# Attention on one core: both score pairs ahead of the value group in the step behind a turn

## The chip, the cores and the metric

The kernel runs on one core of a Trainium2 chip. The metric is the device time of one execution in microseconds (us), the median over several runs. Engines are named as in the profile: PE is TensorE (PEld its weight loads), ACT ScalarE, DVE VectorE, POOL GpSimd, SP SyncE.

## The reference, cut to what matters

The program is a chain of four residual layers on a stream of 4096 tokens of width 256 (two batches of 2048): a linear attention, a mixture of eight experts with two per token, a softmax attention and a second mixture of experts. The change touches only the softmax attention, the third layer:

```python
q = proj_h(v @ Wq.T)            # 16 heads of 16, first component sqrt(1 + |rest|^2)
k = proj_h(v @ Wk.T)
vv = (v @ Wv.T) as heads
sc = (-q0 k0 + q[1:] . k[1:]) / dh ** 0.5
at = softmax(sc, axis=-1)       # over 2048 keys, not causal
out = at @ vv
```

## The kernel before, in words

The function `attention` works on 16 head pairs (two heads of one batch; `NPAIR`, eight pairs for each batch), one after the other. A pair has 32 steps (`ST`): 16 key tiles of 128 keys for the first half of the queries, then the same 16 for the second half. What a step does is called by its place in the loop of L1774:

- `scores(p, step, 0)` and `scores(p, step, 1)` (L1701): two score pairs. Each is two matmuls, one per head on its own half of the rows, 128 keys by 512 queries, into one unit of `psS`, two banks of PSUM. ACT turns each unit into its exponentials (L1800), 128 x 1024 at a time, so 64 in a head pair. In this text exp 20.1 is the one of the second score pair of step 20, and the same for the others.
- `weigh(p, step - 2)` (L1711): the value group, four matmuls side by side in columns of 32 (eight records in the trace), that multiply the exponentials of two steps ago with the values and add them up in `psO`. `pexp` has six buffers, so an exp also waits for the value group that reads the exps of three steps back.
- `means(q, n)` (L1727): one product for the next head pair's shift (an upper estimate of the scores' maximum), which DVE reduces (L1816). It is not there in the last steps of the fifteenth pair and in the sixteenth, since no pair follows.

`psS` has three units (`RING`), given out in turn by the list that `uses` writes (L1577). Three times in a head pair the list puts something else between the scores: behind step 3 the transposed output of the pair before (`turn_out`, L1757; not in the first pair), behind step 19 that of the first half of this pair (`turn_out`), and behind step 28 the transposed shift of the next pair (`turn_shift`, L1750; not in the last pair). These are the turns. `unit_free` (L1691) makes each use wait for the end of what had the same unit three places earlier in the list. For a score pair in a step without a turn that is the score pair three before. In the step behind a turn, the first score pair waits for the first exp of the step before, and the second score pair for the second exp of the step before. `OUT` is (19, 3) and `TURN` 28.

TensorE carries out its instructions in the order of the code, each behind its own wait.

Of the kernel before, what the change touches and what calls it, by code (L numbers as in the profile page):

```python
# [1512 lines left out]
def attention(nc, k):  # L1513
# [18 lines left out]
    TURN = ST - 4  # L1532
    OUT = (KT16 + 3, 3)
# [7 lines left out]
    with Stage(nc, "at") as s:  # L1541
# [53 lines left out]
        def shift_place(p):  # L1595

            bank = psS[:, unit["shift", p, 0], :] if p else psM[:, :]
            return bank.bitcast(F16)[0:ST, 0:P]

        def early(at):  # L1600

            return psS[:, at % RING, :].rearrange("p (h c) -> p h c", h=2)

        def keys(stack, p):
            return stack[:, p % HPAIR, p // HPAIR * TS:(p // HPAIR + 1) * TS]
# [4 lines left out]
        def mean_at(p, step):  # L1610
            return p + 1 + (step + AHEAD) // ST, (step + AHEAD) % ST

        with nc.Block() as block:

            @block.gpsimd
            def _(pool):
                def take_v(p):
                    pool.tensor_copy(vst[:, p % 2, :, :, 0:D],  # L1618
                                     batch(p)[:, :, p % HPAIR * 2 * D:(p % HPAIR + 1) * 2 * D].rearrange("p t (h d) -> p h t d", h=2)
                                     ).then_inc(v_ready, 1)  # L1620

                pool.memset(vst[:, :, :, :, :], 0.0).then_inc(start, 1)
                pool.wait_ge(start, 1)
                pool.memset(vst[:, :, :, :, D:D + 1], 1.0).then_inc(start, 1)
                pool.wait_ge(start, 2)
                def high(c):
                    pool.wait_ge(raw_in[c % SR], (c // SR + 1) * 16)
                    if c >= SR:

                        pool.wait_ge(w_out[c % SR], c // SR * 16)  # L1630
                    pool.tensor_scalar(part(c, 0), raw(c), scale(c), 1.0, ALU.mult, ALU.mult).then_inc(w_high, 1)  # L1631

                take_v(0)
                take_v(1)
                for p in range(2, NPAIR + 1):
                    if p < NPAIR:

                        pool.wait_ge(weighed, 6 + (p - 1) * ST * 2)
                        take_v(p)
                    if p > HPAIR:  # L1640
                        for c in range((p - 1 - HPAIR) * NSP, (p - HPAIR) * NSP):
                            high(c)
# [46 lines left out]
            @block.tensor  # L1689
            def _(pe):  # L1690
                def unit_free(use):  # L1691

                    v = place[use]
                    if v >= RING:
                        kind, p, n = order[v - RING]
                        if kind == "score":
                            pe.wait_ge(raised, p * ST * 2 + n + 1)
                        else:
                            pe.wait_ge(x_free, x_use[kind, p, n] + 1)

                def scores(p, step, n):  # L1701
                    kt, c = step % KT16, step // KT16 * 2 + n
                    use = "score", p, step * 2 + n
                    unit_free(use)
                    for hh in range(2):
                        r = slice(hh * HR, (hh + 1) * HR)
                        mm = pe.matmul(psS[:, unit[use], hh * BANK:(hh + 1) * BANK], keys(k.KT, p)[r, kt * P:(kt + 1) * P],  # L1707
                                       keys(k.QT, p)[r, c * BANK:(c + 1) * BANK], start=True, stop=True)
                    mm.then_inc(scored, 1)

                def weigh(p, step):  # L1711
                    kt, y = step % KT16, step // KT16

                    pe.wait_ge(raised, (p * ST + step) * 2 + 2)
                    if kt == 0:
                        if 2 * p + y:

                            pe.wait_ge(o_out, 2 * p + y)
                        pe.wait_ge(v_ready, p + 1)
                    for g in range(4):  # L1720
                        n, hh = g // 2, g % 2
                        mm = pe.matmul(psO[g * VW:(g + 1) * VW, :], vst[:, p % 2, hh, kt, :],  # L1722
                                       pexp[:, (p * ST + step) % 3 * 2 + n, hh * BANK:(hh + 1) * BANK],
                                       start=(kt == 0), stop=(kt == KT16 - 1))
                    mm.then_inc(weighed, 2)

                def means(p, n):  # L1727
                    if n == 0:
                        pe.wait_ge(k_ready, 4 * (p + 1))
                    if p * ST + n:  # L1730

                        pe.wait_ge(reduced, p * ST + n)
                    hh, t = n % 2, n // 2
                    r = slice(hh * HR, (hh + 1) * HR)
                    pe.matmul(psM[:, :], keys(k.QT, p)[r, t * P:(t + 1) * P], ksumT[r, p % 2, :],  # L1735
                              start=True, stop=True).then_inc(maxed, 1)

                def first_means(p, t):
                    at = p * KT16 + t
                    if t == 0:  # L1740
                        pe.wait_ge(k_ready, 4 * (p + 1))
                    if at >= 3:

                        pe.wait_ge(reduced, 2 * (at - 3) + 2)
                    for hh in range(2):
                        r = slice(hh * HR, (hh + 1) * HR)
                        pe.matmul(early(at)[:, hh, :], keys(k.QT, p)[r, t * P:(t + 1) * P], ksumT[r, p % 2, :],
                                  start=True, stop=True).then_inc(maxed, 1)

                def turn_shift(p):  # L1750
                    pe.wait_ge(shifted, p + 1)
                    if p:
                        unit_free(("shift", p, 0))
                    pe.transpose(shift_place(p), shift[:, :, :].rearrange("p h t -> p (h t)"),
                                 k.identh[:, :]).then_inc(x_turned, 1)

                def turn_out(p, y):  # L1757
                    pe.wait_ge(o_out, 2 * p + y + 1)
                    unit_free(("out", p, y))
                    for c in range(4):  # L1760
                        mm = pe.transpose(psS[:, unit["out", p, y], c * P:(c + 1) * P], oT[:, y, c * P:(c + 1) * P], k.ident[:, :])
                    mm.then_inc(x_turned, 1)

                pe.wait_ge(start, 2)
                for t in range(KT16):
                    first_means(0, t)
                turn_shift(0)
                for t in range(AHEAD // 2):
                    first_means(1, t)

                pe.wait_ge(reduced, ST + AHEAD)
                for p in range(NPAIR):
                    pe.wait_ge(shift_in, 32 * (p + 1))
                    for step in range(ST):  # L1774
                        scores(p, step, 0)
                        if step >= 2:
                            weigh(p, step - 2)
                        elif p:
                            weigh(p - 1, ST - 2 + step)
                        scores(p, step, 1)  # L1780
                        q, n = mean_at(p, step)
                        if q < NPAIR:
                            means(q, n)
                        if step == OUT[1] and p:
                            turn_out(p - 1, 1)
                        if step == OUT[0]:
                            turn_out(p, 0)
                        if step == TURN and p + 1 < NPAIR:
                            turn_shift(p + 1)
                weigh(NPAIR - 1, ST - 2)  # L1790
                weigh(NPAIR - 1, ST - 1)
                turn_out(NPAIR - 1, 1)
# [590 lines left out]
```

## Time and profile before

| | us |
|---|---|
| median of 3 runs | 2340.03 (2338.78 to 2341.39) |
| the profiled execution, its own time | 2340.75 |
| its span | 2339.0 |
| PE busy | 2034.9 (87%) |
| ACT busy | 1513.5 (65%) |
| DVE busy | 1365.6 (58%) |
| exponentials of the attention, L1800, 1024 of them | 942.7 |

The span is what the profile covers; the execution's own time is 1.75 us longer. Times in the rows below are counted from the start of the span. In a row of the timeline several instructions of one kind that follow each other without a gap are merged: the first number is the start of the first, the second the time up to the end of the last, and the count stands behind the x.

### The profile page before, as it was taken

To read this page: it belongs to the slowest core of one execution; us is meant where nothing else is said; L and a number is where in the kernel's file an instruction comes from. 1 tells how busy PE (TensorE), PEld (TensorE's weight loads), DVE (VectorE), ACT (ScalarE), POOL (GpSimd) and SP (SyncE) were. 2 spreads that over 40 slices of the span, in tenths; PEclk is the share of its full clock that TensorE was granted. 3 is DMA by queue.
4 is the path that set the end of the run, shared out by engine and by line. 5 is a ranking of instruction groups with operands and counts; after the bars stand their busy time and mean duration, and the time that the engine had idled before them with its cause. 6 is when DMAs were issued, how large, how long until landed. Compare 5 with 4: busy or idle time off the path is not lost. (4 is left out here: it accounts for less than half of the span.)

```text
span 2339.0 us, 43032 instructions
## 1 busy us (share of the span) xinstructions
PE 2034.9 (87%) x13329; PEld 970.5 (41%) x13330; DVE 1365.6 (58%) x3004; ACT 1513.5 (65%) x2495; POOL 463.8 (20%) x395
## 2 busy tenths in 40 slices
PE   5997799960996999999999999999863699999994
PEld 3786555540662222222222222222252467667663
DVE  5567544438787444444445555554147787777773
ACT  2215333324674999999999999999963344444442
POOL 0030277752000000000000000000000143344341
PEclk9998899985997999999999999999986799999997
DMA  5006377763100000000002222222174477767774
GB/s 200 1 1 225 82 154 152 151 149 154 43 29 1 1 2 1 1 2 1 1 19 73 73 73 73 73 73 73 55 243 148 173 178 174 173 174 174 172 173 129
DMA packets 157317, 225.11 MB, mean 96 GB/s; under 512 B 14080, under 2 KB 130992, under 8 KB 157184
## 3 DMA queue, kind: packets, MB, share of 16 engines
q1 hardware_dynamic: 129376, 184.04, 25.3%
q0 software_dynamic: 27264, 37.24, 9.4%
q10 hardware_dynamic: 544, 2.10, 0.3%
q8 instruction: 78, 1.28, 0.2%
q14 instruction: 55, 0.45, 0.1%
HBM read 157.63 MB, written 65.57 MB: 95 GB/s over the span
## 5 line engine op out<-in xcount | busy, mean ns | idle before, releaser
L1800 ACT ACTIVATE at_pexp<-at_psS 128x1024 f32<-128x1024 f32 x1024 | 942.7, 1163 | 30.7 <-PE at_psS L1707 30.7
L1816 DVE TENSOR_REDUCE at_mx<-at_psM 128x1 f32<-128x512 f32 x474 | 327.3, 691 | 413.8 <-PE at_psM L1735 410.2
L1722 PE MATMUL at_psO<-at_pexp,at_vst 128*32 128x512 f32 x4096 | 546.0, 605 | 3.5 <-ACT at_pexp L1800 0.8
L1707 PE MATMUL at_psS<-l1c_QT,l1c_KT 64*128 64x512 f16 x2048 | 412.7, 385 | 16.2 <-ACT at_pexp L1800 9.8
L1707 PEld LDWEIGHTS at_psS<-l1c_QT,l1c_KT 64*128 64x128 f16 x2048 | 105.4, 93 | 536.5 <-ACT at_pexp L1800 498.6
L2149 PE MATMUL ex_psH<-wide_wgu,ex_xT 128*128 x1278 | 259.9, 357 | 0.6 <-issue 0.6
L986 POOL DMA_INDIRECT sums<-ex_y,top_dst x107 | 170.0, 1589 | 280.1 <-ACT ex_y L2205 226.6
L2220 DVE SCALAR_TENSOR_TENSOR ex_bias<-ex_psH,top_w_scale,ex_bias 128x456 f32<-128x456 f32 x213 | 147.4, 692 | 76.6 <-PE ex_psH L2149 60.3
L2193 ACT ACTIVATE ex_sg<-ex_bias 128x228 f32<-128x228 f32 x213 | 83.7, 393 | 152.3 <-DVE ex_bias L2220 152.3
L972 POOL DMA_INDIRECT ex_xg<-normed,top_tok x142 | 140.1, 987 | 197.6 <-POOLq L81 148.7
L1735 PE MATMUL at_psM<-at_ksumT,l1c_QT 64*128 64x512 bf16 x474 | 178.8, 377 | 0.0
L2149 PEld LDWEIGHTS ex_psH<-wide_wgu,ex_xT 128*128 128x128 f16 x1278 | 124.5, 97 | 112.2 <-issue 4.0
L1722 PEld LDWEIGHTS at_psO<-at_pexp,at_vst 128*32 128x32 f32 x4096 | 81.7, 108 | 186.9 <-issue 120.4
L2172 PE MATMUL ex_psY<-wide_w2h,ex_hT 114*128 x1278 | 151.3, 273 | 1.1 <-DVE ex_y L2247 0.7
L1058 PE MATMUL ex_psH<-l_w,ex_xT 128*128 x284 | 142.7, 626 | 0.0
L1618 POOL COPY at_vst<-wide_x 128x512 f32<-128x512 f32 x16 | 9.7, 610 | 656.4 <-PE at_psO L1722 656.4
L2172 PEld LDWEIGHTS ex_psY<-wide_w2h,ex_hT 114*128 114x128 f16 x1278 | 124.4, 98 | 15.8 <-issue 1.6
L1126 DVE TENSOR_SCALAR ex_y<-ex_psY,top_wgt 128x256 f32<-128x256 f32 x71 | 34.3, 483 | 134.6 <-PE ex_psY L1075 124.5
L1095 ACT ACTIVATE ex_hT<-ex_psG 128x256 f32<-128x256 f32 x71 | 27.2, 383 | 123.0 <-PE ex_psG L1067 123.0
L2205 ACT ACTIVATE ex_y<-ex_y,top_wgt 128x256 f32<-128x256 f32 x71 | 36.1, 508 | 93.7 <-DVE ex_y L2247 93.7
L2231 DVE TENSOR_TENSOR ex_h<-ex_bias,ex_sg 128x228 f32<-128x228 f32 x213 | 82.8, 389 | 11.2 <-ACT ex_sg L2193 11.2
L1631 POOL TENSOR_SCALAR l1c_KT<-l1c_KT,top_w_scale 128x684 f16<-128x684 f32 (+1 forms) x48 | 40.9, 858 | 227.8 <-DMA l1c_KT<-in_L_ffn_W 215.0
(359 smaller groups left out, 2735.8 us busy)
## 6 DMA issues: line engine op xcount, KB each, us to landing
ex_bias<-in_L_ffn_bg SPq DMA_DIRECT2D x71, 342.0 KB, 4.7
ex_bias<-in_L_ffn_b SPq DMA_DIRECT2D x71, 342.0 KB, 5.5
ex_piece<-in_L_ffn_W SPq DMA_DIRECT2D x48, 228.0 KB, 2.7
l1c_KT<-in_L_ffn_W SPq DMA_DIRECT2D x32, 342.0 KB, 3.4
halves<-l1c_KT SPq DMA_DIRECT2D x32, 342.0 KB, 3.2
wide_wgu<-halves SPq DMA_DIRECT2D x8, 1368.0 KB
ex_b<-in_L_ffn_b SPq DMA_DIRECT2D x71, 128.0 KB
normed<-rt_area SPq DMA_DIRECT2D x16, 512.0 KB, 2.6
```

What stands on the lines that cost most here:

```text
L972: pool.indirect_dma_start(xg[:, g, :], None, k.xn_d, bass.IndirectOffsetOnAxis(k.tok[:, t:t + 1].bitcast(U32), 0)).then_inc(got[g], 16)
L986: pool.indirect_dma_start(sums[t % len(sums)], where, y[:, j, :], None, compute_op=ALU.add).then_inc(put[j], 16)
L1058: mm = pe.matmul(psH[:, j, :], xT[:, j, kk, :], k.w13[:, ds(eh, 1), kk, :].rearrange("p a c -> p (a c)"), start=(kk == 0), stop=(kk == KC ...
L1707: mm = pe.matmul(psS[:, unit[use], hh * BANK:(hh + 1) * BANK], keys(k.KT, p)[r, kt * P:(kt + 1) * P], keys(k.QT, p)[r, c * BANK:(c + 1) * ...
L1722: mm = pe.matmul(psO[g * VW:(g + 1) * VW, :], vst[:, p % 2, hh, kt, :], pexp[:, (p * ST + step) % 3 * 2 + n, hh * BANK:(hh + 1) * BANK], s ...
L1735: pe.matmul(psM[:, :], keys(k.QT, p)[r, t * P:(t + 1) * P], ksumT[r, p % 2, :], start=True, stop=True).then_inc(maxed, 1)
L1800: act.activation(pexp[:, u % 6, :], psS[:, unit["score", u // (ST * 2), u % (ST * 2)], :], ACT.Exp, scale=D ** -0.5 / (QS * QS)).then_inc( ...
L1816: dve.tensor_reduce(mx[:, n:n + 1], psM[:, :], AX.X, ALU.max).then_inc(reduced, 1)
L2149: mm = pe.matmul(psH[:, n, 0:G2].rearrange("p (n c) -> p n c", n=2), xT[:, j, x, kk, :], k.wgu[:, ds(e, 1), kk, :, w, n * HW:(n + 1) * HW] ...
L2172: mm = pe.matmul(psY[:, 0:C], hT[:, j, x, g, :], k.w2h[:, ds(e, 1), w, g, :].rearrange("p a c -> p (a c)"), start=(at == 0), stop=(at == l ...
L2193: act.activation(sg[:, n, :], bias[:, st.slot(1, BR), n, 0, :], ACT.Silu).then_inc(gated, 1)
L2220: dve.scalar_tensor_tensor(hb, psH[:, n, 0:G2].rearrange("p (n c) -> p n c", n=2), k.w_scale[:, 1:2], hb, ALU.mult, ALU.add).then_inc(adde ...
```

## The change

In the step behind a turn (`turned`: step 20, step 29, and from the second pair on step 4), the second score pair is issued right behind the first, ahead of the value group. In all other steps the order is as before. Step 29 of the last pair is also reordered, though no turn stands ahead of it: 47 steps in all. Nothing is added or taken away, and the list of units is the same.

```diff
                 for p in range(NPAIR):
                     pe.wait_ge(shift_in, 32 * (p + 1))
                     for step in range(ST):
+                        turned = step - 1 in (OUT[0], TURN) or (step - 1 == OUT[1] and p)
+
                         scores(p, step, 0)
+                        if turned:
+                            scores(p, step, 1)
                         if step >= 2:
                             weigh(p, step - 2)
                         elif p:
                             weigh(p - 1, ST - 2 + step)
-                        scores(p, step, 1)
+                        if not turned:
+                            scores(p, step, 1)
                         q, n = mean_at(p, step)
                         if q < NPAIR:
                             means(q, n)
```

PE in the step behind a turn of the output (here step 20 of the first pair); `at_psS<-l1c_QT,l1c_KT` are scores, `at_psO` the value group, `at_psM` the means product:

```order
 L1735 MATMUL at_psM<-at_ksumT,l1c_QT 128x512
 L1761 MATMUL at_psS<-top_ident,at_oT 128x128 x4
-L1707 MATMUL at_psS<-l1c_QT,l1c_KT 128x512 x2
-L1722 MATMUL at_psO<-at_pexp,at_vst 32x512 x4
-L1707 MATMUL at_psS<-l1c_QT,l1c_KT 128x512 x2
+L1707 MATMUL at_psS<-l1c_QT,l1c_KT 128x512 x4
+L1722 MATMUL at_psO<-at_pexp,at_vst 32x512 x4
 L1735 MATMUL at_psM<-at_ksumT,l1c_QT 128x512
 L1707 MATMUL at_psS<-l1c_QT,l1c_KT 128x512 x2
```

The four score matmuls of the step now stand together, and the value group comes between them and the means product.

PE in the step behind the turn of the shift (step 29 of the first pair):

```order
 L1735 MATMUL at_psM<-at_ksumT,l1c_QT 128x512
 L1754 MATMUL at_psS<-top_identh,at_shift 32x128
-L1707 MATMUL at_psS<-l1c_QT,l1c_KT 128x512 x2
-L1722 MATMUL at_psO<-at_pexp,at_vst 32x512 x4
-L1707 MATMUL at_psS<-l1c_QT,l1c_KT 128x512 x2
+L1707 MATMUL at_psS<-l1c_QT,l1c_KT 128x512 x4
+L1722 MATMUL at_psO<-at_pexp,at_vst 32x512 x4
 L1735 MATMUL at_psM<-at_ksumT,l1c_QT 128x512
 L1707 MATMUL at_psS<-l1c_QT,l1c_KT 128x512 x2
```

The same move behind the one transposition of the shift.

## Rows read from the trace of the kernel before

**Rows 1.** The page, costliest groups: busy, mean ns of one | idle before, releaser.

```profile
L1800 ACT ACTIVATE at_pexp<-at_psS 128x1024 f32<-128x1024 f32 x1024 | 942.7, 1163 | 30.7 <-PE at_psS L1707 30.7
L1816 DVE TENSOR_REDUCE at_mx<-at_psM 128x1 f32<-128x512 f32 x474 | 327.3, 691 | 413.8 <-PE at_psM L1735 410.2
```

**Rows 2.** Timeline of ACT, exp 4.1 of the third pair to 4.0 of the fourth.

```profile
872.12 58.92 ACT L1800 ACTIVATE at_pexp<-at_psS 128x1024 f32<-128x1024 f32 x64 [0.17 <-PE at_psS L1707]
```

**Rows 3.** Timeline of ACT, eighth pair, exp 4.1 alone and exps 4.1 to 19.1.

```profile
1167.58 1.02 ACT L1800 ACTIVATE at_pexp<-at_psS 128x1024 f32<-128x1024 f32 x1 [0.17 <-PE at_psS L1707]
...
1167.58 28.52 ACT L1800 ACTIVATE at_pexp<-at_psS 128x1024 f32<-128x1024 f32 x31 [0.17 <-PE at_psS L1707]
```

**Rows 4.** Timeline of PE, eighth pair, from the turn behind step 19 to step 21.

```profile
1194.41 0.63 PE L1761 MATMUL at_psS<-top_ident,at_oT 128*128 128x128 f32 x4
1195.24 0.39 PE L1707 MATMUL at_psS<-l1c_QT,l1c_KT 64*128 64x512 f16 x2 [0.20 <-ACT at_pexp L1800]
1195.56 1.07 PE L1722 MATMUL at_psO<-at_pexp,at_vst 128*32 128x512 f32 x8
1196.56 0.39 PE L1707 MATMUL at_psS<-l1c_QT,l1c_KT 64*128 64x512 f16 x2
...
1196.79 0.59 PE L1707 MATMUL at_psS<-l1c_QT,l1c_KT 64*128 64x512 f16 x2
1197.31 1.07 PE L1722 MATMUL at_psO<-at_pexp,at_vst 128*32 128x512 f32 x8
1198.31 0.60 PE L1707 MATMUL at_psS<-l1c_QT,l1c_KT 64*128 64x512 f16 x3
```

**Rows 5.** Timeline of ACT there, two exps a row: 18.1 with 19.0, to 21.0 with 21.1.

```profile
1192.89 2.29 ACT L1800 ACTIVATE at_pexp<-at_psS 128x1024 f32<-128x1024 f32 x2
...
1193.80 2.31 ACT L1800 ACTIVATE at_pexp<-at_psS 128x1024 f32<-128x1024 f32 x2
...
1194.70 2.32 ACT L1800 ACTIVATE at_pexp<-at_psS 128x1024 f32<-128x1024 f32 x2
...
1195.67 2.34 ACT L1800 ACTIVATE at_pexp<-at_psS 128x1024 f32<-128x1024 f32 x2
...
1196.99 1.94 ACT L1800 ACTIVATE at_pexp<-at_psS 128x1024 f32<-128x1024 f32 x2
...
1197.91 1.94 ACT L1800 ACTIVATE at_pexp<-at_psS 128x1024 f32<-128x1024 f32 x2
```

**Rows 6.** Timeline around step 29: PE, then ACT (28.0 with 28.1, 30.0 with 30.1).

```profile
1211.82 0.39 PE L1707 MATMUL at_psS<-l1c_QT,l1c_KT 64*128 64x512 f16 x2 [0.51 <-ACT at_pexp L1800]
...
1213.14 0.60 PE L1707 MATMUL at_psS<-l1c_QT,l1c_KT 64*128 64x512 f16 x3
...
1214.89 0.39 PE L1707 MATMUL at_psS<-l1c_QT,l1c_KT 64*128 64x512 f16 x2
...
1210.56 2.12 ACT L1800 ACTIVATE at_pexp<-at_psS 128x1024 f32<-128x1024 f32 x2
...
1214.49 1.94 ACT L1800 ACTIVATE at_pexp<-at_psS 128x1024 f32<-128x1024 f32 x2
```

**Rows 7.** Timeline around step 4: PE, then ACT (2.1 to 3.1, 4.1 to 5.1).

```profile
1165.83 0.39 PE L1707 MATMUL at_psS<-l1c_QT,l1c_KT 64*128 64x512 f16 x2
...
1167.38 0.59 PE L1707 MATMUL at_psS<-l1c_QT,l1c_KT 64*128 64x512 f16 x2
...
1168.90 0.60 PE L1707 MATMUL at_psS<-l1c_QT,l1c_KT 64*128 64x512 f16 x3
...
1163.53 2.97 ACT L1800 ACTIVATE at_pexp<-at_psS 128x1024 f32<-128x1024 f32 x3
...
1167.58 2.85 ACT L1800 ACTIVATE at_pexp<-at_psS 128x1024 f32<-128x1024 f32 x3 [0.17 <-PE at_psS L1707]
```

**Rows 8.** PE by stretches: us, PE busy (count), granted clock, DMA share, GB/s.

```profile
725.00:735.00 10.00, 5.38 (x18) 0.50 0.00 1
760.00:1480.00 720.00, 709.80 (x5182) 1.00 0.09 28
```

## The prediction

> **What bounds the kernel now.** I read the page's costliest groups first, to see which engine is full in the attention stage. The 1024 exponentials of ScalarE (exps) are the largest group, 942.7 us of a span of 2339.0, with 30.7 us idle before them, nearly all of it the wait before the very first one; VectorE spends 410.2 us waiting for means products, so it is not the limit [rows 1]. Then the timeline of ScalarE: a head pair, 64 exps, is one unbroken row of 58.92 us with 0.17 in front, 59.09 in all [rows 2]. How much of that is ScalarE's own pace? A stretch without a turn in it, 31 exps, takes 28.52 us and its first exp 1.02, so 30 ends follow in 27.50: **0.917 us an exp** [rows 3]. 64 of them are 58.67, so a pair loses only 0.42 us, and the stage is bound by ScalarE. Sixteen pairs lose some 6 to 7 us, and that is all that a better order behind the turns could bring.
>
> TensorE is nearly as full. When nothing holds it, step 20 to step 21 goes 1195.56 to 1197.31 between the starts of the value groups, **1.75 us a step**, against 1.83 that two exps take: it gains only 0.08 a step on ScalarE [rows 4]. So whatever TensorE stands still behind a turn, it cannot make good quickly. That is where I look for the effect of the change.
>
> **The place, step 20 of the eighth pair.** The turn sits at the end of step 19 (the transposes at 1194.41). The first score pair of step 20 starts at 1195.24 after 0.20 of waiting for ScalarE, the value group at 1195.56 (+0.32), the second score pair at 1196.56 (+1.00), the next step's first pair at 1196.79 (+0.23; its second half comes 0.21 later, since the row of two covers 0.59 where one covers 0.38), the next value group at 1197.31, the next second pair at 1198.31 [rows 4]. On ScalarE the exps 19.0, 19.1, 20.0, 20.1, 21.0, 21.1 (step and number) end at 1195.18, 1196.11, 1197.02, 1198.01, 1198.93, 1199.85, each the start plus the length of the row that ends with it [rows 5]. Three rules come out of these: a freed score unit lets its pair start 0.06 after the exp's end (1195.18 to 1195.24); an exp that waits starts 0.43 after its score pair (1196.56 to 1196.99) and ends 1.02 after that; and the loss at this turn is 1198.01 - 1197.02 - 0.92 = 0.07, as exp 20.1 waits for a pair that stood behind the value group.
>
> **What the change does there.** A turn takes one of the three units of the ring, so the second pair of the step behind it needs the unit of exp 19.1, not of the exp before. That exp ends at 1196.11. The change puts the pair's wait ahead of the value group, whose own inputs are long there, and TensorE takes its instructions in order.
> - Second pair: 1196.11 + 0.06 = 1196.17 in place of 1196.56. Exp 20.1 is then in time, and the loss of 0.07 goes.
> - TensorE stands still from about 1195.56 to 1196.17. Value group 1196.17 + 0.32 = 1196.49, means and next first pair 1.00 later, 1197.49: **0.70 later** than 1196.79.
> - Its second half is at 1197.70, exp 21.0 starts at 1198.13 and ends at 1199.15, against 1198.93: 0.22 later.
> - The next second pair keeps its distance of 1.52 (1196.79 to 1198.31): 1199.01. Exp 21.1 starts at 1199.44 and ends at 1200.46, against 1199.85: 0.6 later.
> - The second pair of step 22 is at 1199.01 + 1.75 = 1200.76, its exp could start at 1201.19, and ScalarE is ready two starts (1.81) after 1199.44, at 1201.25. So it is in time, and TensorE again wins 0.08 a step. The 0.6 stays lost: **+0.60 at this turn** (the rounding of the rows is some 0.02).
>
> Step 29, behind the turn of the shift: exp 28.1 ends at 1210.56 + 2.12 = 1212.68, so the second pair goes at 1212.74, the value group at 1213.06 and the next first pair at 1214.06; before it was at 1213.37, 0.23 behind 1213.14. That is 0.69 later; the second pair of step 30 goes from 1214.89 to 1215.58, and exp 30.1 ends at 1215.58 + 1.45 = 1217.03, against 1216.43 [rows 6]: **+0.60**.
>
> Step 4, behind the other turn of the output: here TensorE itself is late, its first pair starts at 1165.83, and exp 3.1 ends at 1166.50. Second pair 1166.56, value group 1166.88, next first pair 1167.88 against 1167.38, 0.50 later; second pair of step 5 at 1169.40, exp 5.1 ends at 1170.85 against 1170.43 [rows 7]: **+0.41**. The old loss here, some 0.27 of the pair's 0.42, is traded in, which is why this turn costs less.
>
> **The sum.** Behind the turn of step 19 there are 16 steps, behind that of step 28 there are 15 (the last pair turns no shift), behind that of step 3 again 15 (the first pair has none). One of each kind falls where no means product runs any more, in the last two pairs; there the 0.21 by which a means product delays the next second half is missing, and I take 0.39. So 15 x 0.60 + 0.39 = 9.4; 14 x 0.60 + 0.39 = 8.8; 14 x 0.41 + 0.39 = 6.1. Together **24.3 us**, less a few tenths for rounding: I take 24. The 47th moved group, step 29 of the last pair, has no turn ahead of it and waits one exp less; I cost it at nothing, covered by the 0.08 a step that TensorE has won by then; without this cover it is 0.60.
>
> What else moves: the means product of such a step comes 0.7 later. VectorE waits 410.2 us in all for 474 of them, about 0.9 us each [rows 1], so its reductions and the shift four steps ahead have room: nothing. The exps reuse a buffer that the value group frees: exp 21.0 needs the group that now runs from 1196.49 to about 1197.56 (1.07 long), and starts at 1198.13 anyway. No instruction is added, no DMA queue is passed.
>
> The sum stands against the profiled execution, 2340.75 us (its span and 1.75 around it), so 2364.8 there; the median of the runs is 2340.03, 0.72 below it, and gives **2364.0**.
>
> A larger loss could come from TensorE's clock. In the stretch from 760 to 1480 the granted clock is 1.00, the 2.4 GHz level, although TensorE waits behind each turn, 0.51 us in the longest of the rows shown [rows 4, 6]; between 725 and 735, ahead of the steps, it is busy 5.38 of 10 us and stands at 0.50, the 1.2 GHz level [rows 8]. The waits grow to some 0.6 and 0.5 us, three in 59, so I charge nothing. The Trainium skill (TensorE: Matmul & The Clock Gate, "A second HAM failure mode: psum-queue depth-cycling") says that short idles between matmul groups cycling through PSUM can be frequent enough to make the clock swing between its levels. By that rule the sum would be the one of rival D; the trace of before does not show it.
>
> **The rivals.**
> A, it works as the order suggests (the other side, faster). If the second pair is free to go by 1195.56, right behind the first, nothing stands still, the value group is 0.2 late, and all the losses of before vanish: 0.42 x 15 = 6.3 us, **2333.7**. The point that decides is the end of exp 19.1 against 1195.56. The trace has it at 1196.11, 0.55 too late, and the 0.20 of waiting in front of the first pair shows that units are given back at an exp's end. For it: nothing in the trace but that a semaphore's own time is not shown. 5%.
> B, only the first delay counts: exp 21.0 is 0.22 late, and behind it TensorE catches up in full, so a turn costs 0.2. 46 x 0.2 = 9, **2349**. It needs a faster value group after a wait, and the rows show 1.00 after waits too. 5%.
> C, the full standstill is lost: 46 x 0.69 = 32, **2372**, if TensorE bound the stage throughout or lost more at restart. Against it: the 0.08 a step that it wins. 4%.
> D, the clock falls for about a step behind each turn: a step of 1.75 takes 3.50, 1.67 more than ScalarE's 1.83, 46 x 1.67 = 77 on top of 24, **2441**. 2%.
>
> **How the numbers follow.** The forecast has 84%, and its own range is 2357 to 2369: turns at 0.37 to 0.62 each. The full range reaches down to the edge of B and up to that of C, **2350 to 2371**. A measurement of this kernel tells 0.2%, about 4.7 us, from no change. Faster by more: A, 5%. Within: 3%, if losses and gains meet by an error in the 0.06 or the 0.32. Slower: 92%.
>
> **What would show it.** Right: a row of 64 exps in the timeline of ScalarE takes about 60.7 in place of 59.09, with a wait for scores at the first or second exp two steps behind each turn (5, 21, 30) and none in the step behind it (4, 20, 29); TensorE shows a wait of about 0.6 between the two score pairs of step 20; the granted clock stays 1.00. Wrong: 59.09 or less per row, the second pair 0.32 behind the first, or a wait that is not ScalarE's. If a row is near 59.7 it is B, near 61.2 it is C.

## The result, and the profile after

The changed kernel takes 2365.8 us (median of 5 runs, 2363.64 to 2367.89), the kernel before 2341.14 (5 runs, the three of above among them). The ratio is 1.0108 with a 95% interval of 1.0095 to 1.0121: slower by 24.7 us between the medians. 2364.0 was forecast, in a range of 2350 to 2371. The forecast started from 2340.03, the median of three runs; with five it is 1.1 higher, and that is the larger part of the 1.8 us between 2364.0 and 2365.8.

The costliest groups on the page of the changed kernel (line numbers below the edit are higher by 5):

```profile
L1805 ACT ACTIVATE at_pexp<-at_psS 128x1024 f32<-128x1024 f32 x1024 | 948.5, 1141 | 49.8 <-PE at_psS L1707 49.8
L1821 DVE TENSOR_REDUCE at_mx<-at_psM 128x1 f32<-128x512 f32 x474 | 327.4, 691 | 437.5 <-PE at_psM L1735 433.9
```

Against [rows 1] the exponentials are busy for 5.8 us more and wait for scores for 19.1 us more, together 24.9. VectorE's reductions take what they took and only wait longer. The exps' first and last starts say the same. The view by tile, changed kernel (minimum, median and longest in ns, first and last start in us):

```profile
L1805 ACT ACTIVATE at_pexp<-at_psS x1024: 1017/1117/1492, 744.9 to 1713.5; 128x1024 f32<-128x1024 f32 x171
```

Before:

```profile
L1800 ACT ACTIVATE at_pexp<-at_psS x1024: 1018/1138/1525, 745.7 to 1689.4; 128x1024 f32<-128x1024 f32 x171
```

From the first to the last start it is 968.6 us against 943.7, **24.9 us more**, the whole change. I call this the stretch of the exps. It is the sharper measure in what follows: from profile to profile the rest of the program moves by some us (the first exp starts between 742.8 and 750.0 in the kernels below, all of them the same up to there), while the stretch repeats its pattern pair after pair to a few hundredths.

The timeline of ScalarE, changed kernel, where [rows 2] had one unbroken row for a pair:

```profile
814.44 1.02 ACT L1805 ACTIVATE at_pexp<-at_psS 128x1024 f32<-128x1024 f32 x1 [0.19 <-PE at_psS L1707]
815.75 28.52 ACT L1805 ACTIVATE at_pexp<-at_psS 128x1024 f32<-128x1024 f32 x31 [0.29 <-PE at_psS L1707]
844.46 1.02 ACT L1805 ACTIVATE at_pexp<-at_psS 128x1024 f32<-128x1024 f32 x1 [0.19 <-PE at_psS L1707]
845.78 15.69 ACT L1805 ACTIVATE at_pexp<-at_psS 128x1024 f32<-128x1024 f32 x17 [0.29 <-PE at_psS L1707]
861.64 1.02 ACT L1805 ACTIVATE at_pexp<-at_psS 128x1024 f32<-128x1024 f32 x1 [0.18 <-PE at_psS L1707]
862.97 12.02 ACT L1805 ACTIVATE at_pexp<-at_psS 128x1024 f32<-128x1024 f32 x13 [0.30 <-PE at_psS L1707]
875.18 1.02 ACT L1805 ACTIVATE at_pexp<-at_psS 128x1024 f32<-128x1024 f32 x1 [0.19 <-PE at_psS L1707]
```

The lone exps are 5.0, 21.0, 30.0 and the next pair's 5.0, each the first exp two steps behind a turn. Each waits, and the one behind it (5.1, 21.1, 30.1) waits again. From 814.44 to 875.18, the starts of two exps 5.0, it is 60.74 us a pair; about 60.7 was forecast, 59.09 it was before.

The timeline of TensorE at step 20 of the eighth pair, changed kernel, beside [rows 4]:

```profile
1205.17 0.63 PE L1761 MATMUL at_psS<-top_ident,at_oT 128*128 128x128 f32 x4
1206.00 0.39 PE L1707 MATMUL at_psS<-l1c_QT,l1c_KT 64*128 64x512 f16 x2 [0.20 <-ACT at_pexp L1805]
1206.92 0.39 PE L1707 MATMUL at_psS<-l1c_QT,l1c_KT 64*128 64x512 f16 x2 [0.53 <-ACT at_pexp L1805]
1207.24 1.06 PE L1722 MATMUL at_psO<-at_pexp,at_vst 128*32 128x512 f32 x8
1208.24 0.39 PE L1735 MATMUL at_psM<-at_ksumT,l1c_QT 64*128 64x512 bf16 x1
1208.24 0.59 PE L1707 MATMUL at_psS<-l1c_QT,l1c_KT 64*128 64x512 f16 x2
1208.77 1.06 PE L1722 MATMUL at_psO<-at_pexp,at_vst 128*32 128x512 f32 x8
1209.77 0.60 PE L1707 MATMUL at_psS<-l1c_QT,l1c_KT 64*128 64x512 f16 x3
```

The second score pair follows the first by 0.92, one exp. The view shows 0.53 of idle time in front of it, counted from the recorded end of the first pair; counted from 0.32 behind the start of the first pair, where the value group could go in [rows 4], TensorE stands still for 0.60. The next step's first pair is 2.24 behind the first pair of this step (1208.24 - 1206.00), where it was 1.55 (1196.79 - 1195.24): 0.69 later; 0.70 was forecast. ScalarE there:

```profile
1207.35 1.34 ACT L1805 ACTIVATE at_pexp<-at_psS 128x1024 f32<-128x1024 f32 x1
1208.88 1.02 ACT L1805 ACTIVATE at_pexp<-at_psS 128x1024 f32<-128x1024 f32 x1 [0.19 <-PE at_psS L1707]
...
1210.20 1.02 ACT L1805 ACTIVATE at_pexp<-at_psS 128x1024 f32<-128x1024 f32 x1 [0.29 <-PE at_psS L1707]
```

Exps 20.1, 21.0 and 21.1 end at 1208.69, 1209.90 and 1211.22. Their distances are 1.21 and 1.32 where ScalarE's own pace is 0.917, so 0.29 and 0.40 are lost, and nothing at 20.1 any more. In what follows a loss is always this, the distance of two ends less 0.917.

The clock stayed. TensorE by stretches, as in [rows 8]:

```profile
725.00:735.00 10.00, 5.47 (x18) 0.50 0.00 1
760.00:1480.00 720.00, 695.49 (x5037) 1.00 0.08 26
1480.00:1700.00 220.00, 210.06 (x1522) 1.00 0.23 73
```

### The profile page after: what moved, and what is told of

Read it like the earlier page. It is cut to its first block and busy times, and to the rows that moved or that the text cites. A ratio compares the mean times of both kernels' runs of the same rounds, so it can differ in the third digit from the quotient of the medians.

```text
span 2363.5 us, 43032 instructions
## 1 busy us (share of the span) xinstructions
PE 2034.8 (86%) x13329; PEld 965.2 (41%) x13330; DVE 1369.5 (58%) x3004; ACT 1519.0 (64%) x2495; POOL 464.0 (20%) x395
## 5 line engine op out<-in xcount | busy, mean ns | idle before, releaser
L1707 PE MATMUL at_psS<-l1c_QT,l1c_KT 64*128 64x512 f16 x2048 | 419.8, 384 | 35.2 <-ACT at_pexp L1805 29.4
```

## The experiments

The theory: the second score pair's wait now stands ahead of the value group; TensorE loses 0.69 us behind the turns of steps 19 and 28 and 0.50 behind that of step 3, ScalarE has no such room, and TensorE's surplus of 0.08 a step gives it back too late. The rivals: the new order costs in itself, wherever it stands; the value group, coming later, holds up exps that reuse its buffers, or VectorE's means are late; only the first delay counts.

**1. Only the step behind the turn of step 3.**

```diff
-                        turned = step - 1 in (OUT[0], TURN) or (step - 1 == OUT[1] and p)
+                        turned = step - 1 == OUT[1] and p
```

> Only the step behind the turn of step 3 is reordered (15 steps), steps 20 and 29 are as before. Theory (the second score pair waits for an exp ahead of the value group, and TensorE is late behind it): 14 x 0.41 + 0.39 = 6.1 us, so 2346 to 2347; from the first to the last exp start 949.8 against 943.7 before; losses of ScalarE of 0.29 and 0.40 at exps 5.0 and 5.1, none at 4.1, and 0.08 at 20.1 and 29.1 as before. Rival that a reordered step costs the same everywhere: a third of the whole change, 8 us. Rival that the losses only add up once TensorE is late all along: under 3 us.

Measured: 2347.38 us (10 runs) beside 2340.57 for the kernel before (26), ratio 1.0025 (1.0013 to 1.0036). View by tile:

```profile
L1805 ACT ACTIVATE at_pexp<-at_psS x1024: 1017/1130/1493, 747.3 to 1697.2; 128x1024 f32<-128x1024 f32 x171
```

The stretch is 949.9, 6.2 more than before. Losses are 0.29 and 0.40 at 5.0 and 5.1, none at 4.1, and 0.08 at 20.1 and 29.1 as before. A turn's cost is its own, and the three add up. A third of the whole, 8, is excluded: this turn is cheaper by the 0.27 that it had lost before.

**2. The same order in step 12, which has no turn ahead.**

```diff
-                        turned = step - 1 in (OUT[0], TURN) or (step - 1 == OUT[1] and p)
+                        turned = step == 12
```

> The same reordering, but in step 12 of all 16 pairs, which has no turn in front of it; the steps behind the turns are as before. There the second score pair waits for the exp three uses back, which has ended by then or ends early. Theory: nothing, 2340 to 2341.5, first to last exp start 943.7 to 944.5. Rival (the order itself costs: two score pairs together, or the value group coming late for the exps that reuse its buffer): about 0.6 x 16 = 9.6 us, 2350.

Measured: 2342.4 us (10 runs), ratio 1.0003 (0.999 to 1.0015); the stretch from 749.3 to 1694.2, 944.9, so 1.2 more and not 9.6. At exps 12.0 to 14.1 nothing is lost. So neither the order in itself nor the later value group costs anything on the spot. Nor does a wait as such: the expectation says that the exp three uses back has ended by then, but TensorE does wait for exp 11.0 in step 12 (eleventh pair):

```profile
1361.82 0.39 PE L1707 MATMUL at_psS<-l1c_QT,l1c_KT 64*128 64x512 f16 x2 [0.37 <-ACT at_pexp L1805]
```

The first pair of step 13 is 0.40 later by it than where the end of exp 11.1 would have let it go, and ScalarE loses nothing there. Experiment 6 says why.

The 1.2 is above what I expected, and it lies elsewhere: in seven pairs, from the ninth to the fifteenth, exp 20.1 loses 0.24 instead of 0.08. TensorE in the eleventh pair, steps 18 and 19, this kernel:

```profile
1371.66 0.39 PE L1707 MATMUL at_psS<-l1c_QT,l1c_KT 64*128 64x512 f16 x2
...
1372.78 1.06 PE L1722 MATMUL at_psO<-at_pexp,at_vst 128*32 128x512 f32 x8 [0.30 <-ACT at_pexp L1805]
```

And VectorE there:

```profile
1371.16 0.92 DVE L1873 SCALAR_TENSOR_TENSOR l1c_KT<-l1c_KT,top_w_scale 128x684 f16<-128x684 f32 x1
1372.00 0.68 DVE L1857 COPY at_oT<-at_psO 128x512 f32<-128x512 f32 x1
```

In step 18 the value group begins a new sum in `psO` and waits for VectorE's copy of the old one, which ends at 1372.68 (the view names ScalarE, which had long been done). In these pairs a piece of VectorE's weight splitting (0.92) stands just ahead of that copy, and TensorE was still late from step 12: its value group of step 17 starts 2.10 ahead of the end of exp 17.0 (1372.76), in the kernel before 2.37. A delay that finds no loss where it is made can be paid at the next narrow place.

**3. The means product in the gap.**

```diff
+                        q, n = mean_at(p, step)
                         scores(p, step, 0)
                         if turned:
+                            if q < NPAIR:
+                                means(q, n)
                             scores(p, step, 1)
...
-                        q, n = mean_at(p, step)
-                        if q < NPAIR:
+                        if q < NPAIR and not turned:
                             means(q, n)
```

> As the change, but in the reordered steps the means product stands between the two score pairs, where TensorE waits. Theory: what counts is TensorE's work behind the late release, and 0.21 of it is taken away at each of 43 steps: 9 us less than the change, 2356 to 2357; first to last exp start 959.4 against 968.6. ScalarE's loss at 5.0, 21.0 and 30.0 falls from 0.29 to 0.08, that at 5.1, 21.1 and 30.1 stays 0.40. Rival (the second delay is due to something other than TensorE's queue, such as VectorE's reductions or the value group's buffers): no change, 2365.

Measured: 2356.42 us (5 runs), ratio 1.0056 (1.0034 to 1.0078); the stretch from 746.2 to 1706.5, 960.3. Of that, 0.8 is a loss at exps 2.1 and 3.1 of the first pair, which the change does not have (see the last section); without it 959.5. Timeline of TensorE at step 20 of the eighth pair:

```profile
1203.59 0.39 PE L1707 MATMUL at_psS<-l1c_QT,l1c_KT 64*128 64x512 f16 x2 [0.20 <-ACT at_pexp L1807]
1203.82 0.38 PE L1735 MATMUL at_psM<-at_ksumT,l1c_QT 64*128 64x512 bf16 x1
1204.51 0.39 PE L1707 MATMUL at_psS<-l1c_QT,l1c_KT 64*128 64x512 f16 x2 [0.31 <-ACT at_pexp L1807]
1204.83 1.06 PE L1722 MATMUL at_psO<-at_pexp,at_vst 128*32 128x512 f32 x8
1205.83 0.39 PE L1707 MATMUL at_psS<-l1c_QT,l1c_KT 64*128 64x512 f16 x2
```

The idle time in front of the second pair falls from 0.53 to 0.31, the losses at 5.0, 21.0 and 30.0 from 0.29 to 0.08, and those at 5.1, 21.1 and 30.1 stay 0.40, all as expected: 43 steps by 0.21. The dose answers: what is taken from TensorE's queue behind the late release comes off the time, one to one.

**4. The value group ahead of both score pairs.**

```diff
-                        scores(p, step, 0)
-                        if turned:
-                            scores(p, step, 1)
+                        if not turned:
+                            scores(p, step, 0)
...
-                        if not turned:
-                            scores(p, step, 1)
+                        if turned:
+                            scores(p, step, 0)
+                        scores(p, step, 1)
```

> The third possible order in the same 47 steps: value group, then both score pairs. By the same bookkeeping the first score pair is late by 1.0 less the time that TensorE stood waiting in front of it: exp 20.0 ends 0.5 late, 29.0 about 0.2, 4.0 about 0.87, with the old losses of 0.08, 0.08 and 0.27 traded in, and nothing lost two steps behind. 16 x 0.46 + 15 x 0.14 + 15 x 0.6 = 18.5 us, 2358 to 2359. If only waits between the two score pairs hurt (rival), it costs nothing.

Measured: 2350.09 us (10 runs), ratio 1.0034 (1.0022 to 1.0047); the stretch from 744.4 to 1697.2, 952.8, which is 9.1 more, half of the 18.5 expected. The sign was right and the size was not: 0.40 to 0.48 is lost at 20.0 (0.5 expected), 0.54 at 4.0 (0.87), and at 29.0 **nothing** (0.2). TensorE around step 20:

```profile
1197.14 0.63 PE L1761 MATMUL at_psS<-top_ident,at_oT 128*128 128x128 f32 x4
1197.69 1.07 PE L1722 MATMUL at_psO<-at_pexp,at_vst 128*32 128x512 f32 x8
1198.69 0.61 PE L1707 MATMUL at_psS<-l1c_QT,l1c_KT 64*128 64x512 f16 x4
```

And around step 29:

```profile
1214.04 0.22 PE L1754 MATMUL at_psS<-top_identh,at_shift 128*32 128x128 f16 x1
1214.05 1.06 PE L1722 MATMUL at_psO<-at_pexp,at_vst 128*32 128x512 f32 x8
1215.05 0.39 PE L1707 MATMUL at_psS<-l1c_QT,l1c_KT 64*128 64x512 f16 x2
```

I had let the group start where the row of the transpositions ends. It starts 0.55 behind their start, and 0.01 behind that of the shift's single one, whose rows last 0.63 and 0.22: the recorded end of such a row is not the time from which the next instruction may go. That accounts for steps 20 and 29. The main forecast took TensorE's starts alone and did not suffer from this.

It does not account for step 4, which is half of the miss. There the group gains nothing by it:

```profile
1167.37 0.66 PE L1761 MATMUL at_psS<-top_ident,at_oT 128*128 128x128 f32 x4
1167.96 1.07 PE L1722 MATMUL at_psO<-at_pexp,at_vst 128*32 128x512 f32 x8
1168.96 0.61 PE L1707 MATMUL at_psS<-l1c_QT,l1c_KT 64*128 64x512 f16 x4
```

It starts 0.59 behind the transpositions, as far as the score pair did before (1165.25 to 1165.83). But TensorE comes to this turn earlier: the transpositions start 1.58 ahead of the end of exp 3.1 (1168.95), and before 1.25 ahead (1166.50). These 0.33 are the distance from 0.87 to 0.54. I had carried TensorE's lateness at this turn over from the kernel before, although the steps behind step 28 ran differently.

**5 and 6. Without the turn of step 19, in the order of before and with step 20 reordered.** Both leave out the transposition and division of the first half's output and its place in the list of units, and VectorE's waits are counted accordingly (not shown):

```diff
-                    if step == OUT[0]:
-                        order.append(("out", p, 0))
...
-                        if step == OUT[0]:
-                            turn_out(p, 0)
...
-                        if step == OUT[0]:
-                            divide(p, 0)
```

The second reorders step 20 and no other:

```diff
-                        turned = step - 1 in (OUT[0], TURN) or (step - 1 == OUT[1] and p)
+                        turned = step == OUT[0] + 1
```

> The kernel before without the turn behind step 19: the transposition and the division of the first half's output are left out, and with them its place in the list of units. Its output for the first half of the queries of each batch is therefore not the attention's. Theory: the loss of 0.08 at exp 20.1 goes, 16 x 0.08 = 1.2 us; first to last exp start 942.5 against 943.7.

> The same without that turn, and step 20 reordered in all pairs. Theory: without the turn's place in the ring the second score pair waits for an exp one earlier, and the reordering costs nothing: 942.5 from the first to the last exp start, as without it. Rival (the order itself costs): 9.4 more, 952.

Views by tile, without and with the reordering:

```profile
L1796 ACT ACTIVATE at_pexp<-at_psS x1024: 1018/1245/1765, 750.0 to 1692.1; 128x1024 f32<-128x1024 f32 x171
```

```profile
L1801 ACT ACTIVATE at_pexp<-at_psS x1024: 1017/1230/1680, 742.8 to 1685.5; 128x1024 f32<-128x1024 f32 x171
```

942.1 and 942.7 us, and the 0.6 between them lies at exps 2.1 and 3.1 of the first pair. At steps 20 and 21 neither loses anything. Without the turn's place in the ring, the same reordering of the same step that costs 0.61 in the change costs nothing. (One run each: 2344.91 and 2337.89 us. The first exp starts 7.2 us earlier in the second, ahead of everything that differs, so these two times say nothing of the edit.)

TensorE stands still all the same. The score pairs of step 20 and the first of step 21, eighth pair, in the second of these kernels:

```profile
1191.50 0.39 PE L1705 MATMUL at_psS<-l1c_QT,l1c_KT 64*128 64x512 f16 x2
1192.41 0.39 PE L1705 MATMUL at_psS<-l1c_QT,l1c_KT 64*128 64x512 f16 x2 [0.53 <-ACT at_pexp L1801]
...
1193.74 0.59 PE L1705 MATMUL at_psS<-l1c_QT,l1c_KT 64*128 64x512 f16 x2
```

The wait is the same 0.53, and the next step's first pair is the same 2.24 behind, as in the change. What differs is the exp that ends the wait: 19.0 here, 19.1 there. In the change the way from the end of that exp, over the second pair, the value group and the pairs of step 21, to the end of exp 21.1 takes 4.36 us (1206.86, two exps ahead of the 1208.69 of 20.1, to 1211.22). Four exps take ScalarE 3.67, and the 0.69 between is what it loses. Where exp 19.0 ends the wait, ScalarE has five exps in hand, 4.58, and 0.22 are left over. Experiment 2 is the same case with exp 11.0. So the cost is not TensorE's standing still but how late, by ScalarE's count, the wait is ended.

**7. The turn of step 3 behind step 8, order of before.**

```diff
-    OUT = (KT16 + 3, 3)
+    OUT = (KT16 + 3, 8)
```

> The order of before, with the turn of the second half's output behind step 8 instead of step 3, eleven steps ahead of the next turn and twelve behind the last. Theory: the 0.27 lost at exp 4.1 comes from TensorE's lateness (the turn behind step 28 and a wait in step 2) and falls to the 0.08 of the other two turns: 14 x 0.2 = 2.7 to 2.9 us, 2337.3 median, first to last exp start 940.9. If the loss is of this turn itself it stays: 2340.

```profile
L1800 ACT ACTIVATE at_pexp<-at_psS x1024: 1017/1131/1492, 745.8 to 1687.1; 128x1024 f32<-128x1024 f32 x171
```

The stretch is 941.3, 2.4 less. The 0.27 became 0.08 as expected; in seven pairs (the ninth to the fifteenth) exp 20.1 loses 0.13 instead of 0.08. The median did not follow: 2341.75 (12 runs) beside 2340.44 (17), ratio 1.0 (0.9989 to 1.001), where 2337.3 was expected. The gain shows in the stretch and not in whole runs.

**8. The same, and in step 29 alone the value group first.**

```diff
-    OUT = (KT16 + 3, 3)
+    OUT = (KT16 + 3, 8)
...
-                        scores(p, step, 0)
+                        turned = step - 1 == TURN
+
+                        if not turned:
+                            scores(p, step, 0)
                         if step >= 2:
                             weigh(p, step - 2)
                         elif p:
                             weigh(p - 1, ST - 2 + step)
+                        if turned:
+                            scores(p, step, 0)
                         scores(p, step, 1)
```

> The order of before, with the turn of the second half's output behind step 8, and in step 29 alone the value group ahead of both score pairs. Theory: the 0.27 at exp 4.1 becomes 0.08 at 9.1, and the 0.08 at 29.1 goes, since the single transposition of the shift leaves TensorE time for the value group before the first score pair may start. First to last exp start 940.2, 3.5 us less than before; the median 2336.5 if the rest of the program takes what it took. Rival: step 29 loses 0.1 to 0.4 at exp 29.0, and the stretch is 942 to 946.

```profile
L1805 ACT ACTIVATE at_pexp<-at_psS x1024: 1018/1157/1457, 745.6 to 1686.5; 128x1024 f32<-128x1024 f32 x171
```

The stretch is 940.9, 2.8 less than before and 27.7 less than with the change. The loss at 29.1 is gone in all pairs; 0.6 was added by the first pair's start. 2336.88 us (12 runs) beside 2340.67 (17), ratio 0.9984 (0.9973 to 0.9994): faster than both kernels, by a little. Its median gained more than its stretch and that of experiment 7 less, with stretches only 0.4 apart, so how much of the 3.8 us is the edit's is known from the stretch alone.

**9. The change, with the turn of step 3 behind step 8.**

```diff
-    OUT = (KT16 + 3, 3)
+    OUT = (KT16 + 3, 8)
```

> The change, with the turn behind step 3 moved to behind step 8, and so the reordered step 4 to step 9. Theory: each turn then loses 0.29 + 0.40 two steps behind itself, wherever it stands, because the late release alone sets it; the turn of step 3 was cheap only against its own earlier loss. First to last exp start 968.6, as with the change. Rival: the turn of step 3 costs more because TensorE arrives late there, and moving it saves about 3 us as it did in the order of before: 965.7.

```profile
L1805 ACT ACTIVATE at_pexp<-at_psS x1024: 1018/1125/1525, 744.1 to 1712.7; 128x1024 f32<-128x1024 f32 x171
```

968.6 us, the change's own value (one run, 2363.54 us). 0.29 and 0.41 are lost at 10.0 and 10.1 where it was 0.29 and 0.40 at 5.0 and 5.1. The late release alone sets a turn's price, wherever the turn stands; the 2.4 us that moving it saved in the order of before are no longer there to be saved.

## Why the prediction was right, point by point

- **What bounds the stage.** Right: ScalarE at 0.917 an exp. The stretch is 1023 distances at this pace (27.50 / 30 = 0.9167, so 937.8 us) and the sum of the losses (6.3 before, 31.2 after), to within half a us.
- **The second pair's wait.** Right: exp 19.1 ends it, and TensorE stands still for 0.60, about 0.6 in the forecast. Rival A needed the pair 0.32 behind the first; it came 0.92 behind. That it is the turn's unit which makes the wait cost is shown by experiments 5 and 6: the same order without it has the same wait, ended one exp earlier, and no cost.
- **Why the wait costs.** The chain of the forecast is right: 1196.11 to 1200.46 are 4.35 us, 4.36 measured. The reason given ahead of it, that TensorE can't make good quickly whatever it stands still, is too strong: it stands still just as long in experiment 6, without loss. The 0.08 a step is why two exps lose and no third: from step 22 on the score pairs are in time again.
- **Two delays of 0.29 and 0.40.** Right to a hundredth or two (the forecast's ends, 1199.15 and 1200.46, amount to 0.29 and 0.39). Experiment 3 took 0.21 from the first alone, as it should. Rival B, with the first delay only, is out.
- **The three turns.** 0.60, 0.60 and 0.41 were forecast. By the ends of the exps it is 0.69 - 0.08 = 0.61 twice and 0.69 - 0.27 = 0.42, and for the three without a means product 0.40 and not 0.39. 15 x 0.61 + 14 x 0.61 + 14 x 0.42 + 3 x 0.40 = 24.8, against 24.9 measured. The sum of 24 was a little low because I took the rows' rounding off, where it should have been put on.
- **The 47th group, no cost.** Right: the last pair loses nothing at steps 29 to 31. The cover is another than the 0.08 a step: TensorE waits as long as behind a turn, but exp 28.0 ends the wait, not 28.1. So the change holds its own comparison:

```profile
1708.44 0.39 PE L1707 MATMUL at_psS<-l1c_QT,l1c_KT 64*128 64x512 f16 x2 [0.53 <-ACT at_pexp L1805]
```

- **No cost by buffers or VectorE.** Right for the change: experiment 2 delays both and loses nothing on the spot. But it shows that a delay of 0.4 behind step 12 is still there in part (0.27) at step 17, just ahead of the place where VectorE's copy holds the value group. I had taken the surplus of 0.08 a step as enough without looking for what is met on the way.
- **The clock.** Right: 1.00 from 760 to 1700. The Trainium skill (TensorE: Matmul & The Clock Gate, "A second HAM failure mode: psum-queue depth-cycling") tells of a kernel whose clock swung because TensorE idled briefly and often between matmul groups. It did not swing here, with five waits of 0.20 to 0.53 us in the eighth pair. Rival D is out.
- **Rival C**, the full standstill, would have added 46 x 0.69 = 32 us; 24.9 were added. It came closer than the forecast made it: the new losses are 0.69 at nearly every turn, and only because the old 0.08 or 0.27 comes off is the difference less. But the 0.69 is not TensorE's delay: at step 4 of the eighth pair the next first pair is only 0.50 later against the end of exp 3.1 (1.38 behind it, 0.88 before), and the losses there are the same 0.29 and 0.40.

## What to carry to other kernels

When a wait is moved ahead of other work on an in-order engine, look up in the trace when it is released, and count the time from there to the next result that the bounding engine needs. Then compare that way with what the bounding engine has in hand: 4.36 us against four exps of 0.917 costs 0.69, against five it costs nothing, with the same standstill. Filling the gap with work that is ready, here the value group between the two score pairs, is worth more than having both pairs out early. Where two engines are nearly level (1.75 against 1.83 a step), a delay of one is won back slowly, and what seems hidden where it is made may be paid later, if there is a narrow place within the steps that this takes.

## What the runs showed of the hardware

ScalarE's recorded starts do not show its pace. In an unbroken stretch the starts come closer together than the ends: the longest recorded duration of one and the same 128x1024 exp is 1525 ns, the shortest 1018, while the ends stay 0.917 us apart [rows 3]; and in the kernel without the turn of step 19 it grows to 1765 ns. An exp that had to wait falls back to 1.02. So the mean of 1163 ns [rows 1] says neither what an exp costs nor how long it takes, and losses have to be read between ends.

The first steps of the first pair run while TensorE still has the 1.2 GHz level. How long this goes on differs between kernels that are alike up to there: in the stretch from 750 to 760 the granted clock is 1.00 in the kernel before and 0.91 in experiment 3, which loses 0.8 us at exps 2.1 and 3.1 of the first pair. TensorE by stretches, experiment 3:

```profile
740.00:750.00 10.00, 6.12 (x27) 0.50 0.00 1
750.00:760.00 10.00, 10.00 (x71) 0.91 0.01 2
```

Before:

```profile
740.00:750.00 10.00, 6.65 (x31) 0.55 0.00 1
750.00:760.00 10.00, 10.00 (x78) 1.00 0.01 2
```

In all eleven traces the two go together: in experiments 3, 4, 6 and 8, which lose 0.3 to 0.8 us at exps 2.1 and 3.1, the granted clock rises 4.6 to 5.7 us behind the start of the first exp, and in the seven others, which lose nothing there, 2.7 to 3.4 us behind it. That the clock causes the loss is read from this; it was not tried by itself.
